# A graph layer and a ternary feed-forward layer on one core: h_lo computed by POOL, one down output taken by DVE, and the last node tiles' steps in another order

## The reference, cut to what matters

```
x = x + gnn(layernorm(x))                 # 1250 nodes, 512 features, 20000 edges
  gnn: h = xn @ W_self + mean_over_edges(xn[src] -> dst) @ W_neigh + b
       h = leaky_relu(h, 0.01);  h / max(norm(h), 1e-12)
x = x + ffn(layernorm(x))                 # weights ternary: sign * (scale of the 128-wide group)
  ffn: h = silu(x @ wq_gate.T) * (x @ wq_up.T)        # 512 -> 1408
       h @ wq_down.T                                  # 1408 -> 512
```

## Time and profile before

| | us |
|---|---|
| median of 3 runs (lowest, highest) | 373.68 (373.14, 374.37) |
| the profiled execution | 374.46 |
| its span | 372.7 |

### The profile page before, as it was taken

The page is one execution under the profiler, slowest core; times in us unless marked ns, Lnnn a source line. Parts: engine busy times, 40 slices in busy tenths (PEclk is TensorE's granted clock), DMA queues, the critical chain, the costliest instruction groups (busy, mean ns, idle before and its releaser), DMA issues.

```text
span 372.7 us, 5925 instructions
## 1 busy us (share of the span) xinstructions
PE 340.6 (91%) x1741; PEld 260.3 (70%) x1741; DVE 321.0 (86%) x748; ACT 250.0 (67%) x667; POOL 169.3 (45%) x213
## 2 busy tenths in 40 slices
PE   2988999999999999999776999999999999999961
PEld 1445555555655668777565898989889899889951
DVE  2499999899898428999787899999999999999983
ACT  2164877777667225774556888789788887788730
POOL 3003344242213100110002264888888788788982
PEclk9999999999999999999989999999999999999997
DMA  7941132313222001200000000000000000000035
GB/s 238 288 133 56 60 84 59 85 57 86 56 58 77 25 1 30 77 22 3 0 0 0 2 1 2 0 3 1 2 1 1 2 1 2 0 3 1 0 113 165
DMA packets 9412, 16.70 MB, mean 45 GB/s; under 512 B 1062, under 2 KB 1886, under 8 KB 9378
## 3 DMA queue, kind: packets, MB, share of 16 engines
q1 hardware_dynamic: 9378, 16.29, 15.0%
HBM read 13.73 MB, written 2.56 MB: 44 GB/s over the span
## 4 chain that ended last, share of the span: by engine, by line
PE 60%; DVE 22%; POOL 6%; ACT 6%; issue 4%; POOLq 0%; DVEq 0%; ACTq 0%
PE bank L1172 37%; PE bank L1061 9%; PE bank L1101 5%; DVE hot_dst L877 4%; DVE tq_gu L814 3%; PE bank L1022 3%; POOL acc L590 2%; DVE tq_d L814 2%; ACT mag_early L619 2%; PE bank L456 2%; DVE bn L919 2%; DVE x_sb L916 1%; DVE bn L800 1%; PE bank L1013 1%; DVE z L898 1%
## 5 line engine op out<-in xcount | busy, mean ns | idle before, releaser
L1172 PE MATMUL bank<-x_hi,t_gu 128*128 128x378 f32 (+1 forms) x264 | 96.1, 364 | 3.6 <-DVE x_lo L933 2.8
L1172 PE MATMUL bank<-x_lo,t_gu 128*128 128x378 f32 (+1 forms) x264 | 94.7, 359 | 0.0
L1061 PE MATMUL bank<-w_sb,xnT 128*125 128x512 f32 x160 | 87.4, 634 | 2.2 <-ACT z L649 1.5
L590 POOL TENSOR_TENSOR acc<-acc,d_one 128x378 f32<-128x378 f32 (+1 forms) x84 | 88.2, 1074 | 0.7 <-ACT d_one L725 0.3
L970 DVE SCALAR_TENSOR_TENSOR g_acc<-bank,nscale,g_acc 128x378 f32<-128x378 f32 (+1 forms) x99 | 64.1, 647 | 3.7 <-PE bank L1172 3.2
L552 POOL TENSOR_SCALAR thr<-absum 128x4 f32<-128x4 f32 (+1 forms) x34 | 15.6, 459 | 112.2 <-ACT mag_early L619 79.5
L577 POOL TENSOR_TENSOR hh<-sg,u_acc 128x378 f32<-128x378 f32 (+1 forms) x32 | 35.1, 1098 | 67.5 <-ACT sg L747 63.7
L970 DVE SCALAR_TENSOR_TENSOR u_acc<-bank,nscale,u_acc 128x378 f32<-128x378 f32 (+1 forms) x99 | 63.8, 644 | 0.6 <-PE bank L1172 0.6
L1022 PEld LDWEIGHTS bank<-hot_dst,hot_src 128*125 128x125 bf16 x281 | 32.2, 137 | 39.9 <-issue 22.2
L1172 PEld LDWEIGHTS bank<-x_hi,t_gu 128*128 128x128 f32 x264 | 50.4, 191 | 8.1 <-DVE x_lo L933 3.5
L1172 PEld LDWEIGHTS bank<-x_lo,t_gu 128*128 128x128 f32 x264 | 50.6, 192 | 3.6
(11 more groups left out here) (104 smaller groups left out, 541.7 us busy)
## 6 DMA issues: line engine op xcount, KB each, us to landing
raw<-in_L_ffn_w_gate SPq DMA_DIRECT2D x11, 256.0 KB, 2.6
raw<-in_L_ffn_w_up SPq DMA_DIRECT2D x11, 256.0 KB, 2.6
out_x<-x_sb SPq DMA_DIRECT2D x10, 224.0 KB
raw<-in_L_ffn_w_down SPq DMA_DIRECT2D x8, 256.0 KB, 2.7
x_sb<-in_x SPq DMA_DIRECT2D x1, 1344.0 KB
w_sb<-in_L_gnn_W_neigh SPq DMA_DIRECT2D x1, 1024.0 KB, 5.7
w_sb<-in_L_gnn_W_self SPq DMA_DIRECT2D x1, 1024.0 KB, 6.5
raw<-in_L_ffn_w_down SPq DMA_DIRECT2D x4, 192.0 KB, 2.4
```

Of the source, the lines that this page charges most:

```text
L590: nc.gpsimd.tensor_tensor(to, to, d_one[:, o, slot, 0:width(u)], ALU.add).then_inc(d_added, 1)
L1061: last = nc.tensor.matmul(to[0:TP, :], xnT[:, t, k * TP:(k + 1) * TP], w_sb[:, k, half * D:(half + 1) * D], start=k == 0, stop=k == KD - 1)
L1172: last = nc.tensor.matmul(to, w, parts[h], start=h == 0, stop=h == 1)
```

## The change

- `h_lo` of units 0 to 31 is computed by POOL, between its additions of D1 and D3; DVE keeps it for the last unit, 32.
- D2 is taken by DVE straight into `acc`; ACT and POOL keep D1 and D3. The staging slots of `d_one` are numbered to match. The unit before the last has only D1 by ACT, as before; the last has none.
- T(1,0)'s eight transposes move from the feed-forward stage to the neighbour sums: in pass n = 8 of the loop over the ten sums, after the ninth sum and right after T(0,0)'s, into bank 6. ACT reads them out in turn 0.
- `RING` begins 2, 1, 0 and ends with bank 6, so that bank 6 is first used by the seventh piece (G3 of unit 0), which waits for T(1,0)'s Sign.
- `BANK7`: X8 comes after U1 of unit 1, T(0,1) after U3 of unit 1, X9 after U1 of unit 2.
- In turns 0 to 3 the steps of tiles 7, 8 and 9 on ACT and DVE stand in another order: DVE does `x1_low(7)` before `residual(9)`, `x1_low(8)` after U1 and `shift1(9)` after U2 of turn 1, `x1_low(9)` at the end of turn 2; ACT does `x1_high(8)` before `root_of(9)`, and `normalize1(9)` in turn 1 before the Sign of T(0,1).

```diff
@@ -322,7 +322,7 @@
                 return u in (6, 8, 1, 4)
-            return what in ("G0", "U0") or what in ("D1", "D2", "D3")[:max(0, min(3, NU - 1 - u))]
+            return what in ("G0", "U0") or what in ("D1", "D3")[:max(0, min(2, NU - 1 - u))]
@@ -348,7 +348,7 @@
         index = {p: i for i, p in enumerate(pieces)}
-        RING = [2, 6, 1, 0, 4, 3, 5]
+        RING = [2, 1, 0, 4, 3, 5, 6]
         added = {}
@@ -357,7 +357,7 @@
         for p in added:
-            o = int(p[1][1]) - 1 if p[1] != "O" else len([q for q in stage if q[1] == "O"]) % 3
+            o = {"D1": 0, "D3": 1}[p[1]] if p[1] != "O" else len([q for q in stage if q[1] == "O"]) % 3
             same = [q for q in stage if stage[q][0] == o]
@@ -367,7 +367,7 @@
-        BANK7 = {(0, "U3"): ("X", 7), (1, "U1"): ("T", 1, 0), (1, "U3"): ("X", 8), (2, "U1"): ("T", 0, 1), (2, "U3"): ("X", 9),
+        BANK7 = {(0, "U3"): ("X", 7), (1, "U1"): ("X", 8), (1, "U3"): ("T", 0, 1), (2, "U1"): ("X", 9),
                  (3, "U3"): ("T", 1, 1), (4, "U3"): ("T", 2, 0), (6, "U3"): ("T", 3, 0), (7, "U3"): ("T", 2, 1),
@@ -377,7 +377,7 @@
         through7 = [("T", 0, 0)] + [BANK7[e] for e in sorted(BANK7)]
-        turn_T = {e: i for i, e in enumerate(e for e in through7 if e[0] == "T")}
+        turn_T = {e: i for i, e in enumerate([("T", 0, 0), ("T", 1, 0)] + [e for e in through7[1:] if e[0] == "T"])}
         piece_ready = sem("piece_ready")
@@ -566,6 +566,15 @@
+            def add_down(u, what):
+                p = (u, what)
+                o, slot = stage[p]
+                pool.wait_ge(act_took, took[p])
+                if (before(u), what) in added:
+                    pool.wait_ge(d_added, added[before(u), what])
+                to = acc[:, int(what[1]), nodes_of(u)]
+                nc.gpsimd.tensor_tensor(to, to, d_one[:, o, slot, 0:width(u)], ALU.add).then_inc(d_added, 1)
+
             for n in range(NU + LAG):
@@ -575,19 +584,24 @@
                     nc.gpsimd.tensor_tensor(hh[:, u % 2, 0:w], sg[:, u % 2, 0:w], u_acc[:, u % 2, 0:w], ALU.mult).then_inc(h_done, 1)
-                for u, what in added:
-                    if turn_of[u, what] != n:
-                        continue
-                    p = (u, what)
-                    o, slot = stage[p]
-                    pool.wait_ge(act_took, took[p])
-                    if what == "O":
-                        nc.gpsimd.tensor_tensor(x_sb[:, u, :], x_sb[:, u, :], d_one[0:TP, o, slot, 0:D], ALU.add).then_inc(d_added, 1)
-                    else:
-                        if (before(u), what) in added:
-                            pool.wait_ge(d_added, added[before(u), what])
-                        to = acc[:, o + 1, nodes_of(u)]
-                        nc.gpsimd.tensor_tensor(to, to, d_one[:, o, slot, 0:width(u)], ALU.add).then_inc(d_added, 1)
+                if (n - LAG, "D1") in added:
+                    add_down(n - LAG, "D1")
+                if 1 <= n < NU:
+                    u = n - 1
+                    w = width(u)
+                    pool.wait_ge(hhi_done, u + 1)
+                    if u >= h_slots:
+                        pool.wait_ge(piece_ready, index[u - h_slots, "D0"] + 1)
+                    nc.gpsimd.tensor_tensor(h_lo[:, u % h_slots, 0:w], hh[:, u % 2, 0:w], h_hi[:, u % h_slots, 0:w].bitcast(F32),
+                                            ALU.subtract).then_inc(hlo_done, 1)
+                if (n - LAG, "D3") in added:
+                    add_down(n - LAG, "D3")
+                for p in added:
+                    if p[1] == "O" and turn_of[p] == n:
+                        o, slot = stage[p]
+                        pool.wait_ge(act_took, took[p])
+                        nc.gpsimd.tensor_tensor(x_sb[:, p[0], :], x_sb[:, p[0], :], d_one[0:TP, o, slot, 0:D],
+                                                ALU.add).then_inc(d_added, 1)
@@ -681,14 +695,14 @@
-            def ternary_out(f, down):
+            def ternary_out(f, down, b=7):
...
                 if not down:
-                    nc.scalar.activation(t_gu[:, f % 2, :, :].rearrange("p a d -> p (a d)"), bf(7)[:, 0:2 * D],
+                    nc.scalar.activation(t_gu[:, f % 2, :, :].rearrange("p a d -> p (a d)"), bf(b)[:, 0:2 * D],
                                          ACT.Sign).then_inc(t_done, 1)
@@ -734,12 +748,12 @@
                 if n == 0:
+                    ternary_out(1, 0, 6)
                     normalize1(NT - 2)
...
                 if n == 1:
+                    x1_high(8)
                     root_of(NT - 1)
-                if n == 2:
-                    normalize1(NT - 1)
                 if 1 <= n <= NU:
@@ -754,7 +768,7 @@
                                 act.wait_ge(d_added, added[slot_before[v, what]])
-                            take(v, what, d_one[:, o - 1, stage[v, what][1], 0:width(v)])
+                            take(v, what, d_one[:, stage[v, what][0], stage[v, what][1], 0:width(v)])
                     if what == "D2" and n - 1 > 4 and (n - 1, "U3") in BANK7:
@@ -763,10 +777,9 @@
                 if n == 1:
-                    ternary_out(1, 0)
-                    x1_high(8)
+                    normalize1(NT - 1)
+                    ternary_out(0, 1)
                 elif n == 2:
-                    ternary_out(0, 1)
                     x1_high(9)
@@ -973,6 +986,7 @@
                 dve.wait_ge(hhi_done, u + 1)
+                dve.wait_ge(hlo_done, u)
                 nc.vector.tensor_tensor(h_lo[:, u % h_slots, 0:w], hh[:, u % 2, 0:w], h_hi[:, u % h_slots, 0:w].bitcast(F32),
@@ -983,21 +997,23 @@
                     dve.wait_ge(h_done, u)
+                    dve.wait_ge(hlo_done, u - 1)
                     nc.vector.tensor_tensor(hh[:, u % 2, 0:w], sg[:, u % 2, 0:w], u_acc[:, u % 2, 0:w], ALU.mult).then_inc(h_done, 1)
...
                         take(u, what)
-                    if n == 3 and what == "U1":
-                        x1_low(9)
+                    if n == 1 and what == "U1":
+                        x1_low(8)
+                    if n == 1 and what == "U2":
+                        shift1(NT - 1)
                 if n == 0:
+                    x1_low(7)
                     residual(NT - 1)
-                    x1_low(7)
-                if n == 1:
-                    shift1(NT - 1)
-                    x1_low(8)
-                if 1 <= n <= NU:
-                    low_of_h(n - 1)
+                if n == 2:
+                    x1_low(9)
+                if n == NU:
+                    low_of_h(NU - 1)
                 for t, what in pieces:
@@ -1075,13 +1091,13 @@
-            def ternary_in(f, down):
+            def ternary_in(f, down, b=7):
...
                         for k in range(KD):
-                            last = nc.tensor.transpose(bf(7)[:, a * D + k * P:a * D + (k + 1) * P],
+                            last = nc.tensor.transpose(bf(b)[:, a * D + k * P:a * D + (k + 1) * P],
                                                        tq_gu[:, a * NF + f, k * P:(k + 1) * P], ident_b[:])
@@ -1116,6 +1132,8 @@
                     ternary_in(0, 0)
+                    pe.wait_ge(z_out, NT)
+                    ternary_in(1, 0, 6)
@@ -1135,7 +1153,7 @@
-                    pe.wait_ge(*{2: (block_out, NB), 6: (z_out, NT), 0: (xlo_done, 7), 1: (xlo_done, 6), 4: (hsum, NT - 1),
+                    pe.wait_ge(*{2: (block_out, NB), 6: (t_done, 2), 0: (xlo_done, 7), 1: (xlo_done, 6), 4: (hsum, NT - 1),
                                  3: (squares, NT), 5: (hsum, NT)}[RING[i]])
```

## The result

The changed kernel takes 372.51 us (median of 7 runs, 371.63 to 372.88), the kernel before 373.76 in the same session: ratio 0.996, 95% interval 0.9947 to 0.9972. In a second session it was 372.46 (6 runs) against 374.56 (23 runs), ratio 0.9931 (0.9908 to 0.9954). It is faster; 2.8 us were forecast, 1.25 and 2.1 measured. The two intervals share only 0.9947 to 0.9954, a gain of 1.7 to 2.0 us. The profiled execution took 372.88 us, its span 370.9.

What follows compares the result with a forecast made beforehand. PE was taken to bound the middle, so only its two holes, at the start and at POOL's tail, could give: 1.3 + 1.5 = 2.8 us, 373.68 - 2.8 = 370.9 us. Range over all 369.6 to 373.4.

Steps and rivals of the forecast that it cites:

- signs that it named: Expected in the trace, among others: X9's transposes at 200 to 202 us, one half-clock spell, DVE's last takes 2.8 us earlier.
- forecast case: Start and tail both give and their gains add: 2.8 us less, range 369.7 to 372.1 us, chance 55%.
- rivals A and B: A: only the tail gives, 372.2 us, chance 17%; B: only the start gives, 372.4 us, chance 10%.
- Middle at 0: From 209 to 341 us PE is the bound, so the changes to DVE, ACT and POOL give 0.
- Rival D: Slower: POOL bounds the middle if its `h_lo` costs more than about 2.2 us per turn; 378.4 us, chance 7%.
- T(1,0) at +0.43 before Z: In the neighbour sums, T(1,0)'s eight transposes shift everything by 0.43 us; the same 0.43 us goes later.
- Start, +1.3: PE's first hole, around 183 to 205 us: T(1,1) starts at 207.0 against 208.41 us; gain taken as 1.3 us.
- The lower bound (-0.1): For the start's gain: another slow clock spell like the first costs 1.4 us, which leaves -0.1.
- The X7 to X9 chain: At the start: from X7 at 191.8 us through `residual(9)`, root, silu and Sign to X9 at 200.9, against 204.08.
- ACT's debt: Before T(1,1): ACT owes two rounds, so D1's bank is free at about 206.3 us, wanted at 205.9; stall 0.4 us.
- Tail, +1.5: Last stretch: with less work in turns 29 to 31, POOL ends its last D1 addition at 360.25 us; gain 1.5 us.
- The end after D: After DVE's last four takes begin: transposes, ACT's copy, POOL's addition to x and the final DMA keep fixed lengths.

Runs made afterwards that it cites:

- experiments 2 and 3: Kernel before with the start part alone (the start alone): 373.90 us, ratio 0.9982; with the end part alone: 373.21 us, ratio 0.9957.
- two queues: Changed kernel with the output transfers of tiles 5 and 4 issued by ACT instead of SP: 371.63 us.
- The filler: Changed kernel with 17 more matmuls, values nobody reads, in two PE waits of the start: 370.30 us, ratio 0.9892.
- experiment 9: Tile 6 by DVE: changed kernel with tile 6's output addition taken by DVE instead of ACT's copy and POOL's addition; 371.08 us, ratio 0.9908.

## Why the prediction was right and where it was not

The direction, the places and the mechanisms were right; the forecast of 2.8 us was more than twice the first session's 1.25 us, and 1.3 times what the traces show, 2.10. Of the signs that it named all came, except that DVE's last takes were 2.3 us earlier and not 2.8 (2.1 counted from M). The median, 372.51, lies in the range but above the forecast case's own 372.1, beside the values of rivals A and B. It is neither: both halves gave (experiments 2 and 3).

- Middle at 0: right. PE 132.0 of 132, DVE and ACT lighter, POOL's `h_lo` at 1.007 and 1.280 us, `hh`'s price as taken. Rival D needed more than 2.2 us; with two `h_lo` a turn (2.0 and 2.6 us) POOL is just past the point.
- T(1,0) at +0.43 before Z: measured 0.44.
- Start, +1.3: the mis-sized term. Measured 1.18 - 0.44 = 0.74. The step that failed is "I take the slow spell to end at the same distance": it lasted 6.8 us, and all six pieces, X7's transposes and the next one ran at half clock. In the profile with a 3.4 us spell (two queues, the same code up to D) the start gains 26.15 - 24.30 - 0.44 = 1.41, the 1.4 of the working. The filler shows the cause: without the slow spell the start part gives another 1.87. The lower bound (-0.1) had priced a second spell of this length at 1.4 us; the risk was seen and given too small a chance, and the further 3.4 us then cost 0.67. The premise rested on one profile, and 60 executions of the kernel before show that its short spell was not the usual one. The Trainium skill, "TensorE: Matmul & The Clock Gate", section "HAM oscillation — how this bites in real kernels", describes a kernel of short bursts and longer waits in which PE is throttled again at every wait. Here the clock fell once and stayed low twice as long, and the later waits of 1.45 and 1.49 us brought no second fall.
- The X7 to X9 chain: right in its links; X9 - X7 was to be 9.1, measured 9.41, with X7's four transposes at half clock (1.04 us where 0.6 was taken). ACT's debt stalls PE at 206.65 as forecast (0.4 expected, 0.2 seen).
- Tail, +1.5: measured 1.36. `hh` of unit 31 was on time, better than the 0.2 us late that was expected; what follows on POOL took 9.74 us against 10.0 before. That makes 1.51 on POOL; silu itself ended 0.15 us later, counted from T, and 1.36 is left. The 0.1 to 0.2 us from contention were there too: in turns 29 to 31 the third addition of 504 columns, which overlapped DVE's `h_lo`, took 1.59 to 1.72 us before, the other two 1.26 to 1.28 (4.06 for three); now all take 1.27 or 1.28. DVE pays as well: before, its `h_lo` of 378 columns took 0.54 us on the mean while POOL was idle and 0.83 beside POOL's work. So the 0.66 us that the prediction gives DVE "when it has the memory to itself" is a mean over both, and POOL's 0.93 us is 1.7 times DVE's time alone. The Trainium skill, "GPSIMD Engine Reference", section "Key points", says that GpSimd contends with DVE instructions that have two SBUF inputs. The trace agrees, by these numbers; and DVE's own `hh` of unit 32 fell from 1.40 to 0.90 us.
- The end after D: taken as fixed, and it is (10.76 to 10.84), except where one issue took 1.24 us: 11.41 in the first profile and 11.34 in experiment 9's.
- From trace to median: the 0.78 us between profile and median was treated as an offset. It is within the scatter of single executions (373.14 to 374.37 before), and against such a scatter a gain of 2 us needs more runs than seven to be sized. Between 1.25 and 2.1 each session's times give another answer; the marks give 2.1.

## What to carry to other kernels

Cut every trace at fixed marks and compare stretch by stretch: here that told differences of 0.15 us where times scatter by 2. When an edit takes work out of a gap of PE, ask what the gap does to PE's clock behind it, and whether PE's pace is on the path there; in the new order 6.8 us at half clock cost 1.87 us, in the old one 6.8 us more of it cost 0.13. Do not take a slow spell's length from one profile: the mean clock of every execution is on hand and shows how it varies. Idle PE time in a stretch that hangs on other engines can hold matmuls whose values nobody reads: 17 of them gave back 1.9 us. And where an instruction waits for two engines, read both ends yourself: DVE's rows at D name PE, while POOL's addition ended last.

## What the runs showed of the hardware that was not expected

- With the same code up to D, the half-clock spell was of 3.4 us in one profile (two queues) and of 6.8 in others (the changed kernel, twice; the start alone; tile 6 by DVE). The kernel before ranges from 0.977 to 0.990 in its mean clock. What decides it is open; with PE busy through the gaps there was none at this place, in all three profiles with the filler in the changed kernel.
- One issue among SP's last twelve took 1.24 us instead of 0.32 to 0.43, in two of the changed kernels' profiles (363.14 and 361.91 us), and in each the end came some 0.5 us later after D. Its cause is open.
- Spreading the last issues over two queues gave 0.33 us: the transfers of the six last tiles then keep the DMA engines busy 0.79 of the time from 362 to 366 us.
